# Group 6 of 8 ranked inside the last attention, and the first group's keys of that attention computed in the expert stage in front of it

## The reference

```python
# block 2, feed-forward: each of 8 experts picks its 32 best tokens of every sequence
probs = softmax(x @ gate_w); top_p, top_idx = top_k(probs transposed, 32)
y = gelu(x[top_idx] @ w1) @ w2 * top_p        # 128 -> 512 -> 128, added back at top_idx
# block 3, attention: 16 heads of 8 over ctx, with a key mask
query, key, value = q @ Wq.T + bq, ctx @ Wk.T + bk, ctx @ Wv.T + bv
x = softmax(query key^T / sqrt(8), masked) value, heads joined, @ Wo.T + bo
# block 3, feed-forward: each token goes to its 2 best of 8 experts
topv, topi = top_k(flat @ gate_w + gate_b, 2); topw = softmax(topv)
final = sum over e of topw[e] * (gelu(flat @ W1[e] + b1[e]) @ W2[e] + b2[e])
```

## Time and profile before

| | us |
|---|---|
| median of 3 runs | 1932.45 (1932.33 to 1938.41) |
| the profiled execution | 1928.11 |
| its span, first to last instruction | 1925.7 |
| TensorE busy | 1615.8 (84%) |
| VectorE busy | 1276.1 (66%) |
| ScalarE busy | 1207.2 (63%) |
| POOL busy | 766.4 (40%) |
| mean granted clock of TensorE | 0.916 |

### The profile page before, as it was taken

One profiled execution on the slowest core, in us unless ns is written; L12 is line 12 of the kernel. 1 busy time (PEld: TensorE's weight loads), 2 busy tenths in 40 slices (PEclk: granted clock), 3 DMA queues, 4 the chain that ended last, 5 costly groups with the idle time before them and its releaser, 6 DMA issues. The chain is left out here.

```text
span 1925.7 us, 39053 instructions
## 1 busy us (share of the span) xinstructions
PE 1615.8 (84%) x12652; PEld 1198.1 (62%) x12668; DVE 1276.1 (66%) x3412; ACT 1207.2 (63%) x4191; POOL 766.4 (40%) x736
## 2 busy tenths in 40 slices
PE   4399999689999769999789966899649999849993
PEld 3355555379999636666588955445526666628992
DVE  5599999478888766677557746312346887745554
ACT  2189999089999547878657743333238878813443
POOL 2145555235555541212057836001331445443443
PEclk9799999689999879999989978899769999959996
DMA  3320000110000033333092020100035453342224
GB/s 128 73 109 1 1 1 1 34 45 2 1 1 2 28 99 84 94 89 89 24 299 93 1 88 21 74 0 1 0 109 148 117 160 108 91 159 63 63 60 145
DMA packets 65607, 130.29 MB, mean 68 GB/s; under 512 B 10638, under 2 KB 27073, under 8 KB 63289
## 3 DMA queue, kind: packets, MB, share of 16 engines
q1 hardware_dynamic: 55418, 106.96, 19.0%
q10 hardware_dynamic: 5616, 12.06, 1.9%
q0 software_dynamic: 4384, 8.89, 1.3%
HBM read 92.77 MB, written 52.53 MB: 75 GB/s over the span
## 5 line engine op out<-in xcount | busy, mean ns | idle before, releaser
L599 POOL TENSOR_TENSOR B_E<-B_E,B_r 128x512 f32<-128x512 f32 x256 | 268.0, 1047 | 263.9 <-DVE B_r L581 263.9
L1513 ACT ACTIVATE L_E<-L_sc,L_negm 128x128 f32<-128x128 f32 x1024 | 300.4, 405 | 111.8 <-DVE L_negm L1386 110.7
L593 ACT ACTIVATE B_E<-B_logits,B_m 128x32 f32<-128x32 f32 (+1 forms) x1792 | 364.3, 374 | 9.1 <-DVE B_m L562 8.1
L1386 DVE TENSOR_REDUCE L_negm<-L_sc 128x4 f32<-128x512 f32 x256 | 174.5, 684 | 80.4 <-PE L_sc L1618 71.4
L562 DVE TENSOR_REDUCE B_m<-B_logits 128x16 f32<-128x512 f32 (+1 forms) x256 | 172.6, 675 | 38.0 <-PE B_logits L553 30.7
L1616 PE MATMUL L_sc<-KS,L_QS 128*128 128x512 f32 x256 | 140.7, 550 | 57.4 <-DMA L_QS<-L_qsplit 37.8
L576 DVE TENSOR_REDUCE B_r<-B_E 128x16 f32<-128x512 f32 (+1 forms) x256 | 172.7, 675 | 2.5 <-POOL B_E L599 1.3
L1521 ACT ACTIVATE L_PT<-L_pt 128x512 f32<-128x512 f32 x256 | 167.0, 654 | 0.6 <-PE L_pt L1626 0.6
L551 PE MATMUL B_logits<-B_phihi,B_xhi 128*128 128x512 f32 x256 | 154.0, 601 | 5.1 <-DVE B_philo L538 2.5
L1626 PE MATMUL L_pt<-ident,L_E 128*128 128x128 f32 x1024 | 156.0, 275 | 1.6 <-ACT L_PT L1521 1.6
L1626 PEld LDWEIGHTS L_pt<-ident,L_E 128*128 128x128 f32 x1024 | 122.9, 141 | 23.8 <-ACT L_E L1513 2.1
(11 more groups left out here) (354 smaller groups left out, 3698.6 us busy)
## 6 DMA issues: line engine op xcount, KB each, us to landing
route_rows<-in_F_fill SPq DMA_DIRECT2D x33, 516.0 KB, 19.5
KS<-L_ksplit SPq DMA_DIRECT2D x192, 64.0 KB
L_QS<-L_qsplit SPq DMA_DIRECT2D x42, 256.0 KB
F_xg<-route_rows SPq DMA_DIRECT2D x71, 64.5 KB, 1.9
ew<-in_expert_w SPq DMA_DIRECT2D x1, 4096.0 KB, 15.5
L_cT<-in_ctxT SPq DMA_DIRECT2D x16, 256.0 KB, 4.4
L_ksplit<-L_khi SPq DMA_DIRECT2D x16, 256.0 KB, 2.0
L_ksplit<-L_klo SPq DMA_DIRECT2D x16, 256.0 KB, 2.3
```

Of the source, the lines that this page charges most:

```text
L593: ins = nc.scalar.activation(e[:, cols], self.bank(k)[:, cols], ACT.Exp, bias=self.m[:, k % 4, g:g + 1])
L599: self.st.nc.gpsimd.tensor_tensor(e, e, self.r[:, k % 2, :].unsqueeze(2) .to_broadcast([128, self.ng, self.size]), ALU.mult).then_inc(self ...
L1386: nc.vector.tensor_reduce(negm[:, k % 4, :], sc[k % 2][:].rearrange("p (h k) -> p h k", h=NHG), AX.X, ALU.max, negate=True).then_inc(s["ma ...
L1513: ins = nc.scalar.activation(e[:, h * 128:(h + 1) * 128], sc[k % 2][:, h * 128:(h + 1) * 128], ACT.Exp, bias=negm[:, k % 4, h:h + 1])
```

## The change

- `stage_l2_ffn` loads the key weights, the key bias and group 0 of ctx, and computes the keys of group 0 (TensorE behind the transposes of the probabilities; ScalarE; POOL), writes them to scratch and spreads them into KS[0].
- `stage_attn` with `keyed` leaves these steps out for group 0. The transposes of x now come first, in front of the constant product.
- Group 6 is ranked in the attention: its transposes at the last w = 15, its logits in front of the last output product, its 18 VectorE steps behind the last statistics. POOL completes its rows there; its eight scatters stay in F3, as POOL's first.
- F3 ranks group 7 alone. The eight `initial` products and additions move into the loop, one each in iterations 1 to 8, through one bank.

```diff
@@ stage_attn @@
+    FIRST = [use for use in uses if not (keyed and use == "k")]
+    turn_of = {}
+    for use in (["x", "const"] if keyed else ["const"]) + FIRST:
+        if (use, 0) not in turn_of:
+            turn_of[use, 0] = len(turn_of)
...
-            if route and 0 < n < NG - 1 and w == NORMALISE:
+            if route and n and w == NORMALISE:
                 turn_of["rows", n - 1] = len(turn_of)
-    turn_of["out", NG - 1] = len(turn_of)
+    for use, m in (("logits", NG - 2), ("out", NG - 1), ("ranks", NG - 2)):
+        if route or use == "out":
+            turn_of[use, m] = len(turn_of)
...
+            if keyed:
+                credit(sp, (s["k_put"], 32), (s_kin[0], 16 * 3 * NHG))
...
@@ sync: spread(n) @@
+                if not (keyed and n == 0):
+                    put_keys(n)
+                if n:
+                    sp.wait_ge(s["q_put"], (n + 1) * 32)
+                    spread_q(sp, u)
+
+            def put_keys(n):
...
@@ gpsimd @@
+            if keyed:
+                g.sem_inc(s["k_split"], 1)
+            else:
+                split("k", 0)
...
+            if route:
+                route.complete(g, NG - 2)
             tail.gpsimd(g, NG - 1, (NG - 1) % 2)
...
@@ vector @@
+            if keyed:
+                v.sem_inc(s["k_sum"], 1)
+                v.wait_ge(s["aux_full"], 1)
+                nc.vector.tensor_copy(xnT[:], aux[0][:]).then_inc(free(0), 1)
...
             tail.vector(v, NG - 1, (NG - 1) % 2, steps, None)
+            for w in range(UG):
+                for half in range(2):
+                    route_part(NG - 2, w, half)
...
@@ scalar @@
+            def move_rows(m):
+                t = turn_of["rows", m]
+                a.wait_ge(s["aux_full"], t + 1)
+                if m:
+                    a.wait_ge(s["aux_full"], turn_of["logits", m - 1] + 1)
+                nc.scalar.activation(xrT[:], aux[t % 2][:], ACT.Copy).then_inc(free(t), 1)
...
             for k in range(NU - TURN, NU):
                 move(k)
+            if route:
+                move_rows(NG - 2)
...
@@ tensor @@
+            if keyed:
+                put("x", 0)
+            t.wait_ge(s["w_in"], 16 * NW)
+            t.wait_ge(s["const_ready"], 1)
+            nc.tensor.matmul(aux[turn_of["const", 0]][:, 0:128], bvb[:], W["WoT"][:], start=True, stop=True)\
+                .then_inc(s["aux_full"], 1)
+            if keyed:
+                t.wait_ge(s["c_in0"], 16)
+            for use in FIRST:
+                if not (keyed and use == "x"):
+                    put(use, 0)
...
-                    if route and 0 < n < NG - 1 and w == NORMALISE:
+                    if route and n and w == NORMALISE:
                         put_route("rows", n - 1)
...
+            if route:
+                put_route("logits", NG - 2)
             output(NG - 1)
+            if route:
+                put_route("ranks", NG - 2)
...
@@ stage_l2_ffn @@
+            for dst, src in ((Wk[:], d[key + "_W"][:, 1, :]), (bk[:], d[key + "_b"]),
+                             (rot[1][:].rearrange("p (a d) -> p a d", a=GB), d["ctxT"][:, 0:GB, :])):
+                sp.dma_start(dst, src).then_inc(s["kw_in"], 16)
             sp.dma_start(w1[:], d["F2_w1"]).then_inc(s["w_in"], 16)
             sp.dma_start(w2[:], d["F2_w2"]).then_inc(s["w_in"], 16)
+            sp.wait_ge(s["k_split"], 1)
+            for i, part in enumerate((khi[:].bitcast(F32), rot[0][:])):
+                sp.dma_start(k_d[i], part).then_inc(s["k_put"], 16)
+            sp.wait_ge(s["k_put"], 32)
+            for r, i in enumerate((0, 1, 0)):
+                for h4 in range(NHG):
+                    sp.dma_start(p.KS[0][r * HW + h4 * HD:r * HW + (h4 + 1) * HD, :, h4, :].bitcast(F32),
+                                 k_d[i].rearrange("(g h p) k -> h p g k", g=NHG, h=NHG)[h4]).then_inc(s["k_in"], 16)
+            sp.wait_ge(s["k_in"], 16 * 3 * NHG)
...
+            g.wait_ge(s["k_hi"], 1)
+            nc.gpsimd.tensor_tensor(rot[0][:].bitcast(F32R), rot[0][:], khi[:].bitcast(F32), ALU.subtract).then_inc(s["k_split"], 1)
             g.wait_ge(s["G_ready"], 1)
...
+            a.wait_ge(s["k_ps"], 1)
+            nc.scalar.activation(rot[0][:], hb[0][:], ACT.Identity, bias=bk[:, 1:2]).then_inc(s["k_sum"], 1)
+            a.wait_ge(s["k_sum"], 1)
+            nc.scalar.activation(khi[:], rot[0][:], ACT.Copy).then_inc(s["k_hi"], 1)
...
+                else:
+                    a.wait_ge(s["k_put"], 32)
...
+            t.wait_ge(s["kw_in"], 48)
+            nc.tensor.matmul(hb[0][:], Wk[:], rot[1][:], start=True, stop=True).then_inc(s["k_ps"], 1)
             t.wait_ge(s["rows"], 1)
...
@@ stage_l3_ffn @@
-    LAST = (NG - 2, NG - 1)
+    LAST = (NG - 1,)
...
+            route.scatter(g, NG - 2)
             for m in LAST:
                 route.complete(g, m)
-            for m in LAST:
                 route.scatter(g, m)
...
+                if 1 <= i <= NG:
+                    initial(i - 1)
...
-            for u in range(2):
-                a.wait_ge(s["rows_ps"], u + 1)
-                nc.scalar.activation(xT[u][:], hb[u][:], ACT.Copy).then_inc(s["xT_done"], 1)
+            for m in LAST:
+                a.wait_ge(s["rows_ps"], m - LAST[0] + 1)
+                nc.scalar.activation(xT[m % 2][:], hb[m % 2][:], ACT.Copy).then_inc(s["xT_done"], 1)
...
-                if n >= 2:
-                    t.wait_ge(s["init_used"], n - 1)
-                nc.tensor.matmul(initb[n % 2][:], GT[:, n, :], blk[:], start=True, stop=True).then_inc(s["init_ps"], 1)
-
-            for n in range(NG):
-                initial(n)
+                if n:
+                    t.wait_ge(s["init_used"], n)
+                nc.tensor.matmul(initb[:], GT[:, n, :], blk[:], start=True, stop=True).then_inc(s["init_ps"], 1)
+
             t.wait_ge(s["etab_ready"], 1)
             t.wait_ge(s["w2_in"], 16)
             t.wait_ge(s["w_in"], 32)
-            t.wait_ge(s["init_used"], NG)
...
+                if 1 <= i <= NG:
+                    initial(i - 1)
                 if i >= 2:
                     second(i - 2, expert[i - 2])
```

More of the change, by code:

```diff
@@ L1107, in choose, with stage_attn @@
         return nc.vector.tensor_copy(self.slot[u][:], self.place[u][:])
-def stage_attn(nc, p, d, name, gate, rope, first, route=None):
+def stage_attn(nc, p, d, name, gate, rope, first, route=None, keyed=False):
     uses = ["k", "kr", "x", "q", "qr", "v"] if rope else ["k", "x", "q", "v"]
@@ L1121, in stage_attn @@
     NU = NG * UG
-    turn_of = {("const", 0): 0}
-    for use in uses:
-        turn_of[use, 0] = len(turn_of)
+    FIRST = [use for use in uses if not (keyed and use == "k")]
[3 more added lines that the diff above has]
+            turn_of[use, 0] = len(turn_of)
     for n in range(NG):
@@ L1285, in _ @@
             zero(0)
-            split("k", 0)
+            if keyed:
+                g.sem_inc(s["k_split"], 1)
+            else:
+                split("k", 0)
             split("q", 0)
@@ L1441, in route_part @@
                     v.sem_inc(route.slot_ready, 1)
-            v.wait_ge(s["aux_full"], 1)
-            steps.link(nc.vector.tensor_tensor(gcb[:], aux[0][:, 0:128], bo[:], ALU.add))
-            v.sem_inc(free(0), 1)
+            c = turn_of["const", 0]
+            v.wait_ge(s["aux_full"], c + 1)
+            steps.link(nc.vector.tensor_tensor(gcb[:], aux[c][:, 0:128], bo[:], ALU.add))
+            v.sem_inc(free(c), 1)
             steps.link(nc.vector.tensor_scalar(gcb[:], gcb[:], p.gate[:, gate:gate + 1], None, ALU.mult))
-            for use in uses:
+            for use in FIRST:
                 if use == "v":
@@ L1451, in _ @@
                     nc.vector.memset(VZ[0][:], 0.0).then_inc(s["VZ_zeroed"], 1)
-                take(use, 0)
+                if not (keyed and use == "x"):
+                    take(use, 0)
             nc.vector.memset(VZ[1][:], 0.0).then_inc(s["VZ_zeroed"], 1)
@@ L1521, in move @@
                 nc.scalar.activation(PT[k % 4][:], pt[k % 2][:], ACT.Copy).then_inc(s["pt_moved"], 1)
-            upper("k", 0)
+            if keyed:
+                a.sem_inc(s["k_hi"], 1)
+            else:
+                upper("k", 0)
             upper("q", 0)
@@ L1546, in _ @@
                     if route and n >= 2 and w == 0:
-                        t = turn_of["rows", n - 2]
-                        a.wait_ge(s["aux_full"], t + 1)
-                        if n >= 3:
-                            a.wait_ge(s["aux_full"], turn_of["logits", n - 3] + 1)
-                        nc.scalar.activation(xrT[:], aux[t % 2][:], ACT.Copy).then_inc(free(t), 1)
+                        move_rows(n - 2)
             for k in range(NU - TURN, NU):
                 move(k)
+            if route:
+                move_rows(NG - 2)
         @block.tensor
         def _(t):
-            t.wait_ge(s["w_in"], 16 * NW)
-            t.wait_ge(s["const_ready"], 1)
```

(23 more changed lines are left out.)

10 lines of the change are left out of this document (5 added, 5 removed).

## The result

The changed kernel ran in 1921.45 us (median of 12 runs, 1918.38 to 1924.37), the kernel before beside it in 1931.99 (12 runs, 1924.46 to 1938.41). The ratio of the two is 0.9959, with a 95% interval from 0.9946 to 0.9972: 7.9 us faster, between 5.4 and 10.4. The two medians themselves lie 10.5 us apart, and the two profiled executions 6.3; the text goes by the ratio. The forecast was 1923.5, and faster. That the sum came out near the time is not yet a sign that its terms are right: the largest cost in it was 3.2 us too small, and three small costs did not come.

The account below looks back on a forecast made before the run. TensorE was taken to fill the attention and the last loop, with idle time at two seams. Terms -7.7 + 0.5 + 0.4 + 0.4 - 9.8 + 7.3 = -8.9 us gave 1923.5 us, range 1918.5 to 1929.0.

Parts of the forecast that it names:

- Keys in front: Start of the attention: with the first keys moved to F2, the first score comes 7.7 us sooner.
- the transfers keep their times: Rival, attention's start: the queries' put and spread stay slow, only 3.8 of 7.7 us gained, total -5.0; 10%.
- The clock at the first scores, +0.5: Attention's first scores: TensorE starts at the low clock level and the rise may shift, costing 0.5 us.
- F2, +0.4: Stage F2: the moved key split on POOL may delay VectorE's masks, 0 to 1.3 us, taken as 0.4.
- The end of the attention, +0.4: Seam before F3: group 6's ranking is mostly hidden, costing 0.4 us in all; other end 4.4 + 0.2.
- picks are not hidden: Rival, attention's end: VectorE's 18 steps add in full to the seam, total -4.7 us, 1927.8; 7%.
- the seam's 4 us: Attention's end: POOL is occupied some 4.0 us behind its last operation, until 1699.2, covering the 18 steps ending at 1698.5.
- F3 up to the read, -9.8: F3 before its loop: group 6's scatters start early, so the first rows are read at 25.1, 9.8 us sooner.
- the rival that had them at 1.5 us apart: Rival, F3: scatters stretched beside VectorE's chain and the weights' landing, total -5.8 to -7 us, 1926; 8%.
- The initial products, +7.3: F3's loop: eight products at 0.85 us each plus 0.5 for the first cost 7.3 us, bounds 6.0 to 13.7.
- the rival of +21 us: Rival, F3's loop: products of 32 rows keep the clock low, 6.1 us a tile over seven tiles, 1944.5; 6%.

Follow-up runs that it names:

- e11: The kernel before, unchanged, profiled once more on a third chip, where it took 1928.08 us.
- e10: The changed kernel with twelve further dependent small VectorE steps behind the picks at the attention's end; ran once, in 1920.76 us.
- e5: The changed kernel again without an edit, on a slower chip; ratio 0.9974 to the kernel before.
- e3: The changed kernel with the eight initial products moved behind the loop, in three banks; ratio 0.9917 to the kernel before.
- e6: The changed kernel with the eight initial products in front of the loop again, in three banks; ratio 0.9958 to the kernel before.
- e2: The kernel before with only the routing half of the change, keys as before; ratio 1.0005 to the kernel before.
- e4: The changed kernel with both operands of the initial products filled with zeros from 32 to 128 rows; ratio 0.9933 to the kernel before.
- e8: The changed kernel with the second group's keys before the first score, three initial products in front of the loop and five behind; ratio 0.9899 to the kernel before.
- e9: The kernel of e8 with the four b2 loads issued ahead of the experts' first weights in F3; 1906.34 us, ratio 0.9893 to the kernel before.
- e1: The kernel before with only the keys' half of the change, routing as before; ratio 0.9951 to the kernel before.

## Why the prediction was right or wrong, point by point

**Keys in front: right in its two main steps, and partly luck in the third.** Forecast -7.7, measured -7.7 in the first pair: 3.8 us from the queries' place, 2.8 from their write on an emptier queue, 1.4 from the spread (forecast 0.8), less 0.3 between the sum and the write. The first two are there in every profile. The queries are summed 12.3 to 12.4 us after the start of the stage without the change and 7.7 to 8.6 with it; their spread can go 5.1 to 5.5 us after the second write without it and 2.6 to 2.7 with it. The third is not: the spread took 6.86, 6.52 and 5.50 us in the three profiles without the change and 5.3 to 5.5 in the ten with it. So over the three without (27.9, 27.2, 26.5) and the ten with it (19.3 to 20.2) the gain is nearer to 7.2, and against e11 it is 6.3. The rival that the transfers keep their times, with 3.8, is out.

**The clock at the first scores, +0.5: nothing.** The first sixteen scores have the same distances in both profiles.

**F2, +0.4: nothing.** The wait in front of the mask transposes took in the whole product. The -1.2 us of F2 in the first pair is variation between executions (F2 took 198.4 to 201.6 us in thirteen profiles, 200.1 in e11 without the keys). Without it and without the second group the first pair would give -8.0. That this is near the ratio's 7.9 proves little, since up to 1.4 us of it are the spread of one execution.

**The end of the attention, +0.4: -0.2** (the +2.7 from the first score to F3 without the 2.9 of the second group). Transposes and logits went into the wait for the quotient, and the picks were hidden by the seam. The rival "picks are not hidden" is out. That the seam's 4 us hid them, as the prediction had it, fits e10's reading, but with only 0.2 us to spare; the prediction had 0.7 (1699.2 against 1698.5), without the 1.2 us between VectorE's end and the next stage.

**F3 up to the read, -9.8: -10.3.** Right by its own steps, spacing 1.26 instead of 1.31 us. The scatters were not stretched beside the weights' loads: in all ten profiles with group 6 ranked in the attention POOL issues the last one 21.3 us after the start of F3, so the rival that had them at 1.5 us apart is out. What varies is the time behind it: the read follows at 24.6 us in the first profile and e5, and up to 25.8 in e3 and 26.2 in e6.

**The initial products, +7.3: +10.5. This is the step that failed.** The prediction took the price of a two-pass product of 512 columns from F2, where it follows its like, both with 128 rows. The term was mis-sized: between transposes and products of 128 rows one with 32 costs 1.23 us, while among its like at the full level it costs 0.86 (the first products behind the loop in e3). Seven at 1.23 are 8.6, and the first, with the level rising later, 1.8 (from the first transpose to the third tile 7.3 us, 5.5 before): 10.4. The number lay inside the bounds of 6.0 to 13.7, but it decides the worth of half the change: e2 shows that what the routing half gains in front of the loop the loop takes back. e4 shows which part is the 32 rows, 3 us of the 10.5; the rest is TensorE's time for the products, which was nothing where they stood before.

The Trainium skill, TensorE: Matmul & The Clock Gate, has two rules that bear on this. Its section "Why this matters for your kernels", in the row on small-K matmuls, says that one product of 32 rows takes as long as one of 128. The trace agrees among products of one shape (0.86 us behind the loop in e3, 0.85 in F2) and disagrees for a product between others of 128 rows: 1.23 against 0.86 us. The same page of the Trainium skill, Part 3, section "The mechanism", says that a weight load is pulled ahead of running products if its row group does not conflict or if it goes to the background buffer. The trace agrees where the number of rows stays (the load of F_y is 0.43 us ahead of its product in e4); where it changes, the loads were not ahead, which is where the three gaps of 0.1, 0.2 and 0.1 us lie that vanish in e4. Why a load with another number of rows stays behind, no run here shows.

**The level in the loop.** The third tile ran at the full level, as forecast; the rival of +21 us is out (granted clock 1.00 from 1727 on). What the rival was drawn from shows again where these products stand alone: behind the loop in e3, e8 and e9 the clock fell to 0.50 during the fourth of them, with TensorE listed as busy throughout. With the loop's other work between them it stayed at 1.00.

**Where the sum was right by luck.** Forecast -8.9, ratio -7.9: the loop's 3.2 us too little were met by 0.5 + 0.4 + 0.6 of costs that did not come, 0.4 at the read and 0.3 in the tail, and what is left is the difference of 1 us. And the forecast's -7.7 for the keys met an execution whose spread before was 1.4 us longer than in e11.

**Left open.** Why the queries' spread took 6.86 and 5.50 us in two executions of the kernel before, and why every kernel took some 50 us more in the attention's later groups on two of the chips.

## What to carry to other kernels

A product that was free where the engine waited has a price where the engine is the bound; before it is moved to make room for something else, look for the idle time that is left in front of the full loop and behind it (here 6.7 us and 32 us of TensorE), and for the operand that would come too late for it. Take the price of an operation from a row in which its neighbours have the shape that they will have in the new place. And profile the kernel before twice: two of the differences of this pair, 1.2 and 2.9 us, were nobody's doing, and of a third, the 7.7 us at the first score, up to 1.4.

## What the runs showed of the hardware

- A TensorE product with 32 rows between work of 128 rows cost 1.23 us; the same with zeros up to 128 rows 0.86 (e4), and with 32 rows among its like 0.86 (e3). Where the number of rows changed, the weight load started with its product, and otherwise 0.11 to 0.43 us ahead of it.
- Products of 32 rows alone did not hold the full level: in e3, e8 and e9 the granted clock fell from 1.00 to 0.50 during the fourth of them, with TensorE listed as busy in full.
- At a wait of 2.05 us at the second group the clock fell to its lower level for three microseconds, which cost 1.6 us beyond the wait. It fell in the five executions with waits of 3.1 to 5.4 us too (the 19th score 5.5 to 6.5 us after the 17th), and in none with a wait of 1.45 us or less (3.87 us).
- TensorE waited 0 to 5.4 us for the second group's queries in ten executions of eight kernels whose work up to there is the same but for the first keys.
- Four loads of 4 KB each, issued behind 4 MB on one queue, had their last packets 19.5 to 23.3 us after the start of the stage in twelve executions; issued ahead of them, at 9.1 (e9).
- On two chips, TensorE stood idle inside a run of like products for no reason that the profile names, and the granted clock was lower:

```profile
PE L_pp L1660 <- issue: 14.5, 25, 1.0
```

```profile
1500.00:1700.00 200.00, 164.90 (x1865) 116.39 (x1858) 125.45 (x324) 127.26 (x394) 78.50 (x89) 0.89 0.41 110
```

The first line is from the waits of e1 between 1450 and 1740 (us in total, times, longest), the second a stretch of e5 on the other of the two chips, columns as in the earlier trace rows. In e11, on the third chip, the clock is 1.00 from 1500 to 1680.
